# Cross attention and ternary FFN: the split maxima turned by a DMA transpose instead of by TensorE

## What is computed

```python
q = (layernorm(x) @ Wq).reshape(b, n, 32, 16)
k, v = jnp.split(ctx @ Wkv, 2, axis=-1)
q, k = apply_axial_rope(q, pos), apply_axial_rope(k, pos)
logits = jnp.einsum('bqhd,bkhd->bhqk', q, k) * scale
w = jax.nn.softmax(logits, axis=-1)
attn = jnp.einsum('bhqk,bkhd->bqhd', w, v).reshape(b, n, 512)
x = x + attn @ Wout + bout
x = x + bitlinear(gelu(bitlinear(layernorm(x), w_fc)), w_proj)
```

## Time and profile before

| | |
|---|---|
| median of three runs | 802.71 us |
| profiled execution | 800.98 us, its span 799.1 us |
| TensorE matmuls busy | 773.6 us, 97% |
| VectorE (DVE) busy | 674.0 us, 84% |
| ScalarE (ACT) busy | 462.0 us, 58% |
| GpSimd (POOL) busy | 340.2 us, 43% |
| mean granted clock of TensorE | 0.991 |
| DMA | 116.19 MB, 58.9% of 16 engines' time |

### The profile page before, as it was taken

How to read it: one execution, slowest core, us unless ns; L and a number is a source line. 1 busy time by engine, 2 the same in 40 slices (tenths; PEclk the granted TensorE clock), 3 DMA queues, 4 the chain that set the end, 5 groups by cost and what they waited for, 6 DMA issues and landing times.

```text
span 799.1 us, 11757 instructions
## 1 busy us (share of the span) xinstructions
PE 773.6 (97%) x3844; PEld 332.4 (42%) x3844; DVE 674.0 (84%) x945; ACT 462.0 (58%) x843; POOL 340.2 (43%) x446
## 2 busy tenths in 40 slices
PE   5899999899999999999999999899999999999998
PEld 3788876223322222222222222244444444444443
DVE  7788998788888888888888888269999999998895
ACT  5677775577777777777777777734322333223430
POOL 4787776764355455445445544323222121111000
PEclk9999999799999999999999999999999999999999
DMA  8488996555456555765666583226456644555446
GB/s 286 143 219 240 260 278 154 118 146 137 111 148 173 149 136 143 146 144 156 172 160 173 158 170 84 80 56 139 106 112 142 129 105 93 110 114 106 94 92 132
DMA packets 173743, 116.19 MB, mean 145 GB/s; under 512 B 114626, under 2 KB 145394, under 8 KB 173682
## 3 DMA queue, kind: packets, MB, share of 16 engines
q1 hardware_dynamic: 173682, 115.44, 58.9%
HBM read 64.50 MB, written 25.43 MB: 113 GB/s over the span
## 4 chain that ended last, share of the span: by engine, by line
PE 87%; DVE 6%; ACT 2%; DMA 2%; issue 2%; POOL 1%; SPq 0%; DVEq 0%; POOLq 0%; ACTq 0%
PE banks L723 16%; PE banks L709 15%; PE banks L668 13%; PE banks L977 11%; PE banks L992 11%; PE banks L282 10%; PE banks L963 7%; PE banks L311 2%; PE banks L679 1%; DVE h_stats L1047 1%; ACT probs_words L779 1%; DVE h_scales L1060 1%; PE banks L267 1%; DMA stack_words<-max_rows 1%; DMA stack_words<-stack_words 1%
## 5 line engine op out<-in xcount | busy, mean ns | idle before, releaser
L779 ACT ACTIVATE probs_words<-banks 128x512 f32<-128x512 f32 x512 | 276.2, 597 | 99.9 <-PE banks L709 98.0
L759 DVE TENSOR_REDUCE maxima<-banks 128x2 f32<-128x1024 f32 x240 | 283.1, 1216 | 49.9 <-PE banks L668 49.9
L709 PE MATMUL banks<-stack_words 98*128 98x512 bf16 x512 | 175.0, 385 | 3.7 <-ACT probs_words L779 1.8
L668 PE MATMUL banks<-stack_words 96*128 96x512 bf16 x480 | 144.2, 381 | 0.0
L723 PE MATMUL banks<-probs_words,late_words 128*32 128x512 f32 x1024 | 136.4, 605 | 0.5
L992 PE MATMUL banks<-ternary_words,stack_words 128*128 128x512 f16 x512 | 113.0, 379 | 0.6 <-DMA stack_words<-stack_words 0.6
L977 PE MATMUL banks<-ternary_words,late_words 128*128 128x512 f16 x512 | 113.1, 379 | 0.0
L1155 ACT ACTIVATE probs_words<-probs_words,h_moments 128x2048 f32<-128x2048 f32 (+1 forms) x17 | 32.2, 1901 | 134.4 <-DVE h_moments L1052 134.4
L709 PEld LDWEIGHTS banks<-stack_words 98*128 98x128 bf16 x512 | 39.6, 97 | 144.3 <-ACT probs_words L779 85.1
L796 POOL TENSOR_SCALAR neg_max<-maxima 128x16 f32<-128x16 f32 x32 | 8.3, 258 | 161.7 <-DVE maxima L759 159.9
L992 PEld LDWEIGHTS banks<-ternary_words,stack_words 128*128 128x128 f16 x512 | 50.0, 98 | 64.9 <-issue 6.3
(11 more groups left out here) (145 smaller groups left out, 980.1 us busy)
## 6 DMA issues: line engine op xcount, KB each, us to landing
o_rows<-late_words SPq DMA_DIRECT2D x32, 256.0 KB, 2.7
k_parts<-ternary_words SPq DMA_DIRECT2D x48, 128.0 KB, 3.1
q_parts<-ternary_words SPq DMA_DIRECT2D x48, 128.0 KB, 2.5
stack_words<-q_parts SPq DMA_DIRECT2D x32, 192.0 KB, 2.9
stack_words<-k_parts SPq DMA_DIRECT2D x96, 64.0 KB, 2.7
stack_words<-k_parts SPq DMA_DIRECT2D x32, 192.0 KB, 2.8
attn_words<-in_x_dram SPq DMA_DIRECT2D x16, 256.0 KB, 4.2
probs_words<-in_L_ffn_w_fc_dram SPq DMA_DIRECT2D x16, 256.0 KB, 3.8
```

Source lines behind the costliest of these rows:

```text
L668: mm = self.nc.tensor.matmul(self.score_slot[j % 2][:, i], self.mem.q_stack[0:STACK, slot, head, c * P:(c + 1) * P], self.mem.k_stack[0:ST ...
L709: self.nc.tensor.matmul(self.mem.banks[:, self.ST_BANK[k]], self.mem.k_stack[0:STACK + 2, slot, head, c * P:(c + 1) * P], self.mem.q_stack ...
L759: dve.tensor_reduce(self.maxima[:, g % 2, 2 * j:2 * j + 2], self.score_slot[j % 2], AX.X, ALU.max).then_inc(self.scores_read, 1)
L779: act.activation(self.probs[:, c, head, :], self.mem.banks[:, self.ST_BANK[k]], ACT.Exp, scale=1 / math.sqrt(HEAD)).then_inc(self.exp_done, 1)
```

## The change

`max_parts` is padded from 32 to 128 columns (the pad set to zero once, by GpSimd, at the start), and SP turns it with a DMA transpose of 128 x 128 bfloat16 into `max_rows`, which has 128 partitions now; `load_max` reads the first 32. TensorE's turn, ScalarE's copy and the second identity are gone. The banks 4 to 6 hold turned scores alone, in one ring of three that runs on from group to group. On SP the new `turn_max` of group s - 2 comes first in step s, ahead of `load_stacks`; it waits for the split maxima of that group. `load_weight` moves from the head of the step to a place behind `load_max`, and on GpSimd `split_maxima` comes ahead of `ternarise`.

```diff
         self.ident = sb("ident", [P, P], F32)
-        self.identb = sb("identb", [P, P], BF16)
         self.ternary_words = sb("ternary_words", [P, GROUPS * DIM // 2], F32)
...
-    HALFWAY = 8
     EARLY = 2
     SINGLES = EARLY * GH * CHUNKS
-    RING = [4 + i % 3 for i in range(15)] + [5, 6]
-    TURN_BANK = RING[HALFWAY]
-    ST_BANK = RING[:HALFWAY] + RING[HALFWAY + 1:]
+    ST_BANKS = 3
...
         self.neg_max = sb("neg_max", [P, 2, GH * CHUNKS], F32)
-        self.max_parts = sb("max_parts", [P, 2, 2 * GH * CHUNKS], BF16)
-        self.max_rows = sb("max_rows", [2 * GH * CHUNKS, 2, P], BF16)
+        self.max_parts = sb("max_parts", [P, 2, P], BF16)
+        self.max_rows = sb("max_rows", [P, 2, P], BF16)
         self.score_slot = [banks[:, 0:2], banks[:, 2:4]]
         self.early_bank = banks[:, 7]
-        self.early_max_bank = banks[0:2 * GH * CHUNKS, 1, CTX:CTX + P // 2].bitcast(BF16)
         self.pv_bank = banks[:, 7]
-        st = self.ST_BANK
-        self.st_before = [max(j for j in range(k - 16, k) if st[j % 16] == st[k]) for k in range(16)]
-        self.before_turn = max(k for k in range(self.HALFWAY) if st[k] == self.TURN_BANK)
-        self.after_turn = min(k for k in range(self.HALFWAY, 16) if st[k] == self.TURN_BANK)
-        self.max_bank = banks[0:2 * GH * CHUNKS, self.TURN_BANK, 0:P // 2].bitcast(BF16)
+        self.st_bank = [banks[:, 4 + i] for i in range(self.ST_BANKS)]
...
         self.max_loaded = [sem(f"max_loaded_{i}") for i in range(STACK_SLOTS)]
+        self.max_turned = [sem(f"max_turned_{i}") for i in range(2)]
         self.inverse_loaded = [sem(f"inverse_loaded_{i}") for i in range(2)]
...
         self.rows_set = sem("rows_set")
+        self.max_padded = sem("max_padded")
         self.scores_ready = sem("scores_ready")
...
         self.split_ready = sem("split_ready")
-        self.max_turned = sem("max_turned")
-        self.max_saved = sem("max_saved")
         self.st_ready = sem("st_ready")
...
+    def turn_max(self, sp, g):
+        sp.wait_ge(self.split_ready, g + 1)
+        sp.wait_ge(self.max_padded, 1)
+        if g >= 2:
+            sp.wait_ge(self.max_loaded[(g - 2) % STACK_SLOTS], ((g - 2) // STACK_SLOTS + 1) * DMA)
+        sp.dma_start_transpose(self.max_rows[:, g % 2], self.max_parts[:, g % 2]).then_inc(self.max_turned[g % 2], DMA)
+
     def load_max(self, sp, g):
-        sp.wait_ge(self.max_saved, g + 1)
+        sp.wait_ge(self.max_turned[g % 2], (g // 2 + 1) * DMA)
         sp.dma_start(self.mem.q_stack[STACK:STACK + 2, g % STACK_SLOTS].rearrange("p h (c q) -> p (h c) q", c=CHUNKS),
-                     self.max_rows[:, g % 2]).then_inc(self.max_loaded[g % STACK_SLOTS], DMA)
+                     self.max_rows[0:2 * GH * CHUNKS, g % 2]).then_inc(self.max_loaded[g % STACK_SLOTS], DMA)
...
         if g == self.EARLY and j == 0:
-            pe.wait_ge(self.max_saved, 1)
+            pe.wait_ge(self.prj.x_low_ready, TILES)
+            pe.wait_ge(self.prj.ctx_low_ready, TILES)
         if g == self.EARLY and j == 1:
...
-    def turn_first_max(self, pe):
-        pe.wait_ge(self.split_ready, 1)
-        self.nc.tensor.transpose(self.early_max_bank, self.max_parts[:, 0], self.mem.identb[:]).then_inc(self.max_turned, 1)
-
-    def turn_max(self, pe, g):
-        pe.wait_ge(self.split_ready, g + 1)
-        if g > 0:
-            pe.wait_ge(self.exp_done, (g - 1) * 16 + self.before_turn + 1)
-        self.nc.tensor.transpose(self.max_bank, self.max_parts[:, g % 2], self.mem.identb[:]
-                                 ).then_inc(self.max_turned, 1)
-
     def scores_turned(self, pe, g, k):
...
                 pe.wait_ge(self.prj.rest_done[side], TILES)
-        if k != self.after_turn:
-            need(pe, self.exp_done, g * 16 + self.st_before[k] + 1)
-        elif g < GROUPS - 1:
-            pe.wait_ge(self.max_saved, g + 2)
-        else:
-            pe.wait_ge(self.exp_done, g * 16 + self.before_turn + 1)
-        self.nc.tensor.matmul(self.mem.banks[:, self.ST_BANK[k]],
+        need(pe, self.exp_done, g * 16 + k + 1 - self.ST_BANKS)
+        self.nc.tensor.matmul(self.st_bank[(g * 16 + k) % self.ST_BANKS],
                               self.mem.k_stack[0:STACK + 2, slot, head, c * P:(c + 1) * P],
...
                 self.scores(pe, s, 2 * c + 1)
-            if c == 1 and s <= GROUPS:
-                self.turn_max(pe, s - 1)
...
             need(act, self.pv_done, (g - 1) * CHUNKS + c + 1)
-        act.activation(self.probs[:, c, head, :], self.mem.banks[:, self.ST_BANK[k]], ACT.Exp,
+        act.activation(self.probs[:, c, head, :], self.st_bank[(g * 16 + k) % self.ST_BANKS], ACT.Exp,
                        scale=1 / math.sqrt(HEAD)).then_inc(self.exp_done, 1)
-
-    def save_max(self, act, g):
-        act.wait_ge(self.max_turned, g + 1)
-        if g >= 2:
-            act.wait_ge(self.max_loaded[(g - 2) % STACK_SLOTS], ((g - 2) // STACK_SLOTS + 1) * DMA)
-        act.copy(self.max_rows[:, g % 2], self.max_bank if g else self.early_max_bank).then_inc(self.max_saved, 1)
...
         pool.tensor_scalar(self.neg_max[:, r], self.maxima[:, r], -1.0, None, ALU.mult).then_inc(self.neg_ready, 1)
-        need(pool, self.max_turned, g - 1)
+        need(pool, self.max_turned[r], g // 2 * DMA)
         pool.wait_ge(self.neg_ready, g + 1)
...
                     att.load_stacks(sp, (8, 10, 13, 15).index(s))
                 if s == TILES + 3:
+                    att.turn_max(sp, 0)
                     att.load_max(sp, 0)
             for pair in range(2):
...
             for s in range(GROUPS + 3):
-                if 2 <= s < GROUPS:
-                    att.load_weight(sp, w_fc, w_proj, s)
+                if 1 <= s - 2 < GROUPS:
+                    att.turn_max(sp, s - 2)
                 if STACK_SLOTS <= s < GROUPS:
                     att.load_stacks(sp, s)
...
                 if 1 <= s - 2 < GROUPS:
                     att.load_max(sp, s - 2)
+                if 2 <= s < GROUPS:
+                    att.load_weight(sp, w_fc, w_proj, s)
                 if within(s - 2, GROUPS):
                     att.turn_weight(sp, s - 2)
...
         def _(pe):
-            pe.wait_ge(filled, 4)
+            pe.wait_ge(filled, 2)
             prj.turn_positions(pe)
...
                     prj.project_k(pe, s - 3)
-                if s == TILES + 2:
-                    att.turn_first_max(pe)
                 if s >= 10:
...
                     prj.second_part(act, s - 4, 1)
-                if s == TILES + 2:
-                    att.save_max(act, 0)
...
                         att.exponentials(act, s - 2, k)
-                    if k == att.HALFWAY - 1 and within(s - 1, GROUPS):
-                        att.save_max(act, s - 1)
                     if k == 3 and s == GROUPS + 1:
...
         def _(pool):
-            for n, square in enumerate((mem.ident, mem.identb)):
-                pool.memset(square[:], 0.0).then_inc(filled, 1)
-                pool.wait_ge(filled, 2 * n + 1)
-                pool.affine_select(out=square[:], in_=square[:], compare_op=ALU.not_equal, fill=1.0, base=0,
-                                   pattern=[[-1, P]], channel_multiplier=1).then_inc(filled, 1)
+            pool.memset(mem.ident[:], 0.0).then_inc(filled, 1)
+            pool.wait_ge(filled, 1)
+            pool.affine_select(out=mem.ident[:], in_=mem.ident[:], compare_op=ALU.not_equal, fill=1.0, base=0,
+                               pattern=[[-1, P]], channel_multiplier=1).then_inc(filled, 1)
             pool.memset(prj.row_ones.bitcast(mybir.dt.uint32), 0x3F803F80).then_inc(prj.row_ones_set, 1)
             pool.memset(mem.half_power[:], -0.5).then_inc(prj.power_set, 1)
+            pool.memset(att.max_parts[:, :, 2 * GH * CHUNKS:P], 0.0).then_inc(att.max_padded, 1)
             pool.wait_ge(prj.power_set, 1)
...
                     att.stage_v(pool, s - 1)
+                if 2 <= s < GROUPS:
+                    att.split_maxima(pool, s)
                 if s < GROUPS:
                     att.ternarise(pool, s)
-                if 2 <= s < GROUPS:
-                    att.split_maxima(pool, s)
                 if s >= 10 and s % 2 == 0:
...
             pool.wait_ge(rows.bout_loaded, DMA)
```

## The result

The changed kernel takes 872.42 us (median of 5 runs, 869.37 to 873.36) against 800.83 in the same comparison: 1.088 times as long, 95% interval 1.0853 to 1.0905. The forecast was 833, its range 800 to 850. The sign and the mechanism came as forecast; the time is 39 us above the forecast and 22 above the range.

What follows compares the result with a forecast made beforehand. TensorE, busy 97% of the span, was taken as the bound. 800.98 - 8.2 (turns) - 0.4 (old stall) + 27.6 (new stalls) + 12 (clock) = 832.0, with 1 us towards the median 833; range 800 to 850 us.

Steps and rivals of the forecast that it cites:

- The stalls, 27.6 us in the sum: TensorE waiting for late maxima rows at the end of 12 steps with quotient loads, 2.3 us each: 27.6 us lost.
- The turns, 8.2 us: Attention loop on TensorE: 31 turns of the maxima gone, 0.265 us each, 8.2 us gained.
- The wait at the head of SP's step and what is queued behind it: SP waits for the split maxima, delaying stack loads, store, quotient loads and rows load; TensorE stands 1.4 to 3.15 us.
- Turn at T + 2.5: SP issues the DMA turn when the split ends, 2.5 us after T, the start of TensorE's step.
- L641 at T + 8.05: Second quotient load on SP starts 8.05 us after TensorE's step begins (T), against 4.44 before: a shift of 3.6 us.
- The landing, 4.7 to 6.4 us after L641: Quotients, and the maxima rows load held behind them, land 4.7 to 6.4 us after the second quotient load starts.
- The clock, 12 us: TensorE's clock falls to half after 7 of 12 stalls, a little over 3 us each: 12 us lost.
- The upper bound, 20: Clock loss if it falls after all 12 stalls, 1.7 us of work each: 20 us.
- the prediction's own rival for both at their bounds, 851: Stalls of 3.15 us with the clock falling after each: 851 us; chance 10%.
- Steps without quotient loads, 0: Maxima rows in the alternate steps: a TensorE stall between 0 and 0.95 us, taken as 0.
- Rival 1, the load not held: The 8 KB maxima rows load passes beside the quotient loads and TensorE does not wait: 793 us, faster; chance 12%.

Runs made afterwards that it cites:

- the kernel with both orders: Changed kernel with SP's stack loads ahead of the DMA turn and the maxima rows load ahead of the two quotient loads: 796.44 us, 0.9923 of before.
- the filled stalls: Changed kernel with 14 more matmuls, their result overwritten, ahead of TensorE's wait for the maxima rows in every second step, groups 7 to 29: 837.03 us.
- the wait alone: Kernel before, TensorE's turn kept, with only SP's wait for the split maxima put ahead of the stack loads: 826.55 us.
- the shifted stream: Changed kernel with 64 more small transposes on TensorE at its very start, one step's worth of instructions: 857.75 us.
- the eighth of the bytes: Changed kernel with the two quotient loads cut to an eighth of their bytes, every instruction where it was: 801.90 us.
- either of two exchanged lines: Changed kernel with SP's turn moved behind the stack loads, 796.97 us (0.9944); or with the maxima rows load moved ahead of the quotient loads, 796.23 us (0.9928).

## Why the prediction was right in kind and wrong in size

The mechanism came as forecast; two terms of the sum were too small. The stalls, 27.6 us in the sum, were 48.4, and the clock's loss, 12, was 27.8. Together these are 36.6 of the 37.4 us by which the profiled execution (869.37) lies above the sum (832.0). The stalls were too small in two of their parts, the start of L641 and the landing behind it.

- *The turns, 8.2 us:* right in the loop. Step 11.35 us, quarters 2.84; the kernel with both orders, 1.7 us of stalls left in it, is 7.35 us faster in the profiled executions and 6 us by the medians of its comparison (802.39 and 796.44).
- *The wait at the head of SP's step and what is queued behind it:* right, in which steps (12) and on what TensorE waits. Turn at T + 2.5, as worked out. The step where the forecast failed is the next one, **L641 at T + 8.05**: it was T + 9.1 in the mean. The durations were those of a step in which no instruction load fell among the stack loads; the sum was right for such steps to 0.24 us (T + 8.29), and ten of twelve were others. The trace of before already had it: the one old stall lies in a step that begins at 311.29 (the prediction has 311.1), and L641 comes 1.3 us later in it than in the earlier trace rows, since the stack loads there took 1.6 us longer with a q8 load among them. The prediction read that stall for the transfer's length alone.
- *The landing, 4.7 to 6.4 us after L641:* mis-sized too. It was read from two steps, and the 4.7 from the flow of bytes; by the completions of the rows load it is 5.0 in that step, 5.0 to 7.2 and 5.8 in the mean in all twelve of the kernel before, and after the change 6.4. So 9.11 + 6.43 is T + 15.54, 4.03 after the end of TensorE's step at T + 11.51. Of the 1.78 us by which the stall was taken too small (4.03 for the 2.25 that T + 8.05 and the middle of the landing give), 1.06 is L641's start and 0.88 the landing, less 0.16 for the end of the step.
- *The clock, 12 us:* mis-sized, 27.8 by the clock's records and 26.2 by the steps behind the stalls and by the filled stalls. It was taken to fall after 7 of 12 stalls of 2.3 us for a little over 3 us each. At 4 us it fell after 11, and mostly for twice that stretch. The upper bound, 20, allowed no stretch longer than the one that the earlier trace rows shows, though the trace of before has a longer one, 10.24 us from 140.19 on, in the slice that stands at 7 in the earlier trace rows (two stretches of it below; granted clock third from last). With stalls of 1.5 us (the wait alone) it fell after 3 of 12, with 3.1 us (the shifted stream) after 11, but mostly for 3.4 us. The two terms are not independent, and the prediction's own rival for both at their bounds, 851, was too low in each.

```profile
143.60:147.00 3.40, 1.83 (x6) 0.81 (x6) 1.72 (x4) 0.72 (x1) 1.45 (x5) 0.50 0.87 197
147.00:150.43 3.43, 3.43 (x10) 1.21 (x8) 2.96 (x6) 2.17 (x4) 3.24 (x4) 0.50 0.31 69
```

- *Steps without quotient loads, 0:* right, though a rows load lands as late as T + 12.75 there. Such a step is itself 1.6 to 3.1 us longer, at the half clock.
- *Rival 1, the load not held:* refuted by the stalls, and the eighth of the bytes shows what holds it. How it comes about that the load is held at a DMA share of 0.6 can be argued from the completions: the semaphore of the rows load of the step at 396.64 counts up once at 407.50, then twice, at 411.89 and 411.90, and that of the two quotient loads once early and eight times late for each, 409.60 to 412.44. I read this as two DMA engines for the rows load and eight for each quotient load. The Trainium skill (DMA: Bandwidth & Descriptors, section "Why a DMA increments its semaphore by 16 and not by 1") states just this pattern: a copy uses the largest number of engines up to 16 that divides the slowest dimension on both of its sides, on SP's queue the lowest-numbered ones, and the rest of the count of 16 is written at once. By that rule the two engines of the rows load are always among the eight of the quotient loads, while the other eight carry neither; the trace agrees in the counts. No view here names the engines, so the sharing itself is not shown.

## What to carry to other kernels

Before a wait is put at the head of an in-order DMA queue, follow the small load that is issued last and needed first: what counts is which large loads are still under way ahead of it when it goes out. Put such a load ahead of the large ones that nobody awaits yet; either of two exchanged lines turned 9% slower into 0.6 to 0.7% faster here. And where a stall of TensorE is forecast, take its length from all the steps that the trace has, and price the clock with it and not beside it.

## What the runs showed of the hardware

- TensorE's instruction loads lengthen the issue of DMAs on SP: in the changed kernel the stack loads of a stalled step take 3.0 us without one among them and 3.6 to 4.3 us with one, and moving TensorE's instructions by one step took them all to 3.0. Their number follows TensorE's instructions: 31 for 3844 matmuls, 30 for 3812, 32 for 3980. With the turn gone, a step is 64 matmuls and as many weight loads, so two steps hold 256 instructions, and the load came at the same place of every second step; with the turn it wandered. The Trainium skill (Runtime: NRT & Kernel Launch, section "Instruction fetch mechanics") states that an engine refills in blocks of 256 instructions; the trace agrees (16 KB packets, one in two steps). It calls the refill mostly hidden, which holds for TensorE here (its steps take 11.35 us with one or without) but not for SP. Why SP's issue gets longer is open.
- In the changed kernel the granted clock fell for 3.41 or 6.83 us after a stall, in a loop that is otherwise at full clock. Stalls of up to 1.44 us in the kernel with the wait alone passed without it, and so did one of 1.94 there and one of 2.22 in the changed kernel; with the turn behind the stack loads it fell after one of 1.47. Why one stall costs twice as long a stretch as another is open too.
- The DMA transpose of 128 x 128 takes SP 1.12 us to issue, hardly less than the 1.22 of 128 x 512, and lands 2.2 to 4.6 us after its issue, 3.2 in the median.
